# Maximum stage of a graph kernel: positions one group ahead, the other stages one group further behind the messages

## The reference

```python
ew = 1.0 / (pos[src] - pos[dst])
def _graph_conv(x, src, dst, ew, W_rel, b_rel, W_root):
    msg = x[src] * ew[:, None]
    agg = jax.ops.segment_max(msg, dst, num_segments=N)
    agg = jnp.where(jnp.isfinite(agg), agg, 0.0)
    return agg @ W_rel.T + b_rel + x @ W_root.T
```

## Time and profile before

| what | us |
|---|---|
| median of three timed runs | 6097.28 |
| the profiled execution | 6076.85 |
| its span | 6075.1 |
| busy in the span: TensorE | 3609.1 |
| VectorE | 3319.1 |
| GpSimd | 2684.2 |
| ScalarE | 1849.9 |

### The profile page before, as it was taken

The page is one execution under the profiler, slowest core; times in us unless marked ns, Lnnn a source line. Parts: engine busy times, 40 slices in busy tenths (PEclk is TensorE's granted clock), DMA queues, the critical chain, the costliest instruction groups (busy, mean ns, idle before and its releaser), DMA issues. The chain is left out here.

```text
span 6075.1 us, 87448 instructions
## 1 busy us (share of the span) xinstructions
PE 3609.1 (59%) x18318; PEld 2628.9 (43%) x18319; DVE 3319.1 (55%) x10385; ACT 1849.9 (30%) x4701; POOL 2684.2 (44%) x2677
## 2 busy tenths in 40 slices
PE   1455555555554454577214997995666666666664
PEld 0444454455532222244001554654555555555552
DVE  6666666666664444587001333225666666666668
ACT  0444444444422222243000000003444444444442
POOL 1555555555526666601774000005555455454524
PEclk9855555555566676687556998997777777777776
DMA  5555555556531111123103885644333333333331
GB/s 116 182 183 190 186 182 188 185 181 194 185 106 50 49 49 49 49 90 84 22 0 64 200 191 186 196 140 115 87 85 84 83 85 85 84 86 82 87 85 33
DMA packets 822107, 695.48 MB, mean 114 GB/s; under 512 B 538545, under 2 KB 717733, under 8 KB 808431
## 3 DMA queue, kind: packets, MB, share of 16 engines
q1 hardware_dynamic: 552746, 449.58, 24.9%
q0 software_dynamic: 97584, 175.68, 10.8%
q10 hardware_dynamic: 171540, 68.00, 4.7%
HBM read 510.64 MB, written 108.55 MB: 102 GB/s over the span
## 5 line engine op out<-in xcount | busy, mean ns | idle before, releaser
L2362 POOL DMA_INDIRECT ring<-xl_rows,idx x880 | 893.0, 1015 | 1681.1 <-DVE idx L2542 861.6
L435 POOL DMA_INDIRECT ringa<-x_sign_pos,idxa x880 | 864.7, 983 | 691.5 <-DVE msga L600 385.0
L987 POOL DMA_INDIRECT edge_counts<-edge_cnt,places x832 | 828.1, 995 | 733.9 <-issue 262.9
L520 PE MATMUL sela<-hota,endsa 128*128 128x128 f32 x1760 | 425.0, 417 | 482.6 <-ACT endsa L461 400.7
L1905 PE MATMUL pss<-x3s,mats 128*128 128x385 bf16 x2401 | 452.5, 340 | 355.3 <-issue 349.3
L2487 PE MATMUL zps<-xr,hotT 128*128 x2640 | 384.2, 254 | 381.1 <-DVE z L2561 212.6
L520 PEld LDWEIGHTS sela<-hota,endsa 128*128 128x128 f32 x1760 | 365.1, 307 | 500.5 <-issue 430.6
L2500 PE MATMUL ops<-val,hot 128*128 128x200 f32 x1760 | 469.6, 417 | 141.9 <-issue 125.5
L2683 DVE TENSOR_TENSOR out<-out,ops 128x200 f32 x880 | 317.9, 361 | 415.5 <-remote 277.0
L2489 PE MATMUL zps<-We,eaT 128*128 128x128 f32 x1760 | 495.3, 367 | 63.0 <-issue 62.4
L2487 PEld LDWEIGHTS zps<-xr,hotT 128*128 128x128 bf16 x2640 | 271.8, 114 | 492.1 <-issue 458.8
(11 more groups left out here) (388 smaller groups left out, 6591.7 us busy)
## 6 DMA issues: line engine op xcount, KB each, us to landing
edge_counts<-zeroa SPq DMA_DIRECT2D x55, 1568.0 KB
matd<-edge_counts SPq DMA_DIRECT2D x12, 6272.0 KB
keyb<-edge_keys SPq DMA_DIRECT2D x50, 1216.0 KB
reseta<-resets SPq DMA_DIRECT2D x110, 512.0 KB
dstba<-dst_in_tile_bf ACTq DMA_DIRECT2D x112, 256.0 KB
dstb<-dst_in_tile_bf SPq DMA_DIRECT2D x110, 256.0 KB
eaT<-in_eaT SPq DMA_DIRECT2D x880, 32.0 KB
val<-in_ea ACTq DMA_DIRECT2D x880, 32.0 KB
```

Of the source, the lines that this page charges most:

```text
L435: p.indirect_dma_start(out=ring[:, k, :], out_offset=None, in_=table, in_offset=bass.IndirectOffsetOnAxis(ap=idx[:, k:k + 1], axis=0)).the ...
L520: ins = t.matmul(sel[q % 2][:, k * P:(k + 1) * P], ends[:, q % 2, k, :], hot[:, q, k, :], start=True, stop=True)
L987: p.indirect_dma_start(out=g.M.rearrange("d s -> (d s)").unsqueeze(1), out_offset=bass.IndirectOffsetOnAxis(ap=g.place[:, c:c + 1], axis=0 ...
L2362: p.indirect_dma_start(out=ring[:, q % GR, k, :], out_offset=None, in_=g.xl_rows[0:N, :], in_offset=bass.IndirectOffsetOnAxis(ap=idx[:, (q ...
```

## The change

All stages behind the messages move one group further back: in step G, TensorE selects for G-4 (before G-3), transposes the messages of G-2 (G-1) and transposes back G-3 (G-2); VectorE adds G-5 (G-4), scans G-3 (G-2) and loads the tile numbers of G-4 (G-3); the `hot` masks are made for G-1 (G); ScalarE copies G-3 (G-2). The positions of a group are computed by TensorE one step earlier, G+1 in step G, between the message transposes and the transposes back. The gathers, the messages, the distances and the signs stay in their steps. Two turns instead of one stand outside TensorE's and VectorE's loops, and one step more follows VectorE's.

```diff
--- before.py
+++ after.py
@@ -416,6 +416,12 @@
             zero = m.sb(f"zero{tag}", [P, NT * P], BF16)
             s_zero, s_clear = m.sem(f"s_zero{tag}"), m.sem(f"s_clear{tag}")
 
+        def late_turns(eng, body):
+            for it in range(2):
+                body(it)
+            with eng.Fori(2, TURNS) as it:
+                body(it)
+
         with nc.Block() as block:
             @block.gpsimd
             def _(p):
@@ -494,10 +500,10 @@
                             ins = s.activation(sgn[:, q % 2, k, :], ring[:, q * GS + k, F:2 * F], ACT.Copy,
                                                scale=zs[:, q % 2, k:k + 1])
                         ins.then_inc(s_sg, 1)
-                        if not (isinstance(it, int) and q < 2):
-                            ends_of(G - 2, (q - 2) % NG)
+                        if not (isinstance(it, int) and q < 3):
+                            ends_of(G - 3, (q - 3) % NG)
                 turns(s, body, TURNS)
-                for b in (2, 1):
+                for b in (3, 2, 1):
                     ends_of(TURNS * NG - b, NG - b)
                 for h in range(2):
                     s.wait_ge(s_b[h], 16 * (TURNS + 1))
@@ -543,17 +549,18 @@
                 def body(it):
                     for q in range(NG):
                         G = it * NG + q
-                        positions(G, q)
-                        for lag, stage in ((3, select), (1, transposed), (2, back)):
-                            if not (isinstance(it, int) and q < lag):
+                        for lag, stage in ((4, select), (2, transposed), (-1, positions), (3, back)):
+                            if not (isinstance(it, int) and G < lag):
                                 stage(G - lag, (q - lag) % NG)
-                turns(t, body, TURNS)
+                positions(0, 0)
+                late_turns(t, body)
                 GL = TURNS * NG
-                select(GL - 3, NG - 3)
-                transposed(GL - 1, NG - 1)
-                back(GL - 2, NG - 2)
+                for b in (2, 1):
+                    select(GL - b - 2, (-b - 2) % NG)
+                    transposed(GL - b, NG - b)
+                    back(GL - b - 1, (-b - 1) % NG)
+                select(GL - 2, NG - 2)
                 back(GL - 1, NG - 1)
-                select(GL - 2, NG - 2)
                 select(GL - 1, NG - 1)
 
             @block.vector
@@ -607,24 +614,21 @@
 
 
                     G = it * NG + q
-                    first = isinstance(it, int) and it == 0
-                    on = lambda lag: lag >= last and not (first and q < lag)
+                    on = lambda lag: lag >= last and not (isinstance(it, int) and G < lag)
                     at = lambda lag: (G - lag, (q - lag) % NG)
-                    new, adds, msgs = on(0), on(4), on(1)
+                    new, adds, msgs = on(0), on(5), on(1)
                     if adds:
                         A = [v.snap(r, min_val=0, max_val=NT - 1) for r in aregs]
                         for k in range(GS):
-                            add(*at(4), k, A)
-                    if new:
-
-                        wait(v, s_sel, G - NG + 1)
-
-                        v.tensor_tensor(hot[:, q, :, :], bc_mid(g.iota_n[:, :], GS),
-                                        bc_last(g.dend[:, bass.ds(G * GS, GS)], P), ALU.is_equal).then_inc(s_hot, 1)
-                    if on(2):
-                        scan(*at(2), it if q >= 2 else it - 1, ((q - 2) % NG) // 2)
+                            add(*at(5), k, A)
+                    if msgs:
+                        wait(v, s_sel, G - NG)
+                        v.tensor_tensor(hot[:, (q - 1) % NG, :, :], bc_mid(g.iota_n[:, :], GS),
+                                        bc_last(g.dend[:, bass.ds((G - 1) * GS, GS)], P), ALU.is_equal).then_inc(s_hot, 1)
                     if on(3):
-                        load_tiles(G - 3)
+                        scan(*at(3), it if q >= 3 else it - 1, ((q - 3) % NG) // 2)
+                    if on(4):
+                        load_tiles(G - 4)
                     if new:
                         v.wait_ge(s_at, G + 1)
                         v.tensor_reduce(posd[:, :], where[q % 2][:, 0:3 * GS].rearrange("p (k i) -> p k i", i=3), AX.X, ALU.add
@@ -657,8 +661,8 @@
                 def body(it):
                     for q in range(NG):
                         step(it, q)
-                turns(v, body, TURNS)
-                for q in range(4):
+                late_turns(v, body)
+                for q in range(5):
                     step(TURNS, q, q + 1)
```

## The result

The changed kernel took 6139.82 us (four runs, 6135.24 to 6153.99) beside 6096.74 us for the kernel before (four runs): a ratio of 1.0079, 95% interval 1.006 to 1.0097 (intervals below are of the same kind). It is slower by 0.8%, where 5997 us and "faster" were forecast. The time lies inside the range and on the other side of no change.

The account below looks back on a forecast made before the run. Waits on late TensorE results, no full engine, were taken to bound the Maximum stage. Groups of 6.44 to 6.92 us gave -158 to -53 us, middle -105, +5 for drain and code: 5997 us from 6097.28; range 5880 to 6185 us.

Parts of the forecast that it names:

- What bounds the kernel: Maximum stage: no engine fills the 7.14 us a group; VectorE waits 2.05 us; TensorE's late back transposes cost 1.5 us.
- Margins on VectorE: Most of VectorE's 209.2 us wait before positions and 75.0 us before the scan goes, perhaps half of the additions' wait.
- all four signs: VectorE waits: positions under 60 us, scan near 0, the rest before additions; ScalarE's idle before copying back in the hundreds.
- Lateness carried over unchanged: Delay from back's drawn end on TensorE until its result is usable, taken as 1.5 us a group after the change too.
- The sum: Maximum stage: TensorE's recurring cycle 4.94 us plus 1.5 us of late results, 6.44 us a group, -158 us in all.
- bad case: Back, now last in TensorE's step, late by 1.98 us a group: 6.92 us a group, -53 us in all.
- Positions ahead of back: On TensorE, position matmuls enter the recurring cycle ahead of back, adding 0.29 us a group.
- calm cycle: Copy, select, transposes, back, next copy when nothing is late: 4.65 us before, 4.94 us forecast after the change.
- The slower one: Rival, chance 0.22: GpSimd's gathers hold TensorE's results; margins lengthen runs to twelve, 7.55 us a group, +86 us, 6183 us.
- Everything hidden: Rival, chance 0.12: TensorE waits less and runs more at 2.4 GHz; 5.3 us a group, -409 us, 5690 us.
- No change: Rival, chance 0.16: back late by 2.1 to 2.3 us a group eats the other gains; within 18 us of 6097.

Follow-up runs that it names:

- lag_only: The changed kernel with the positions of G back at the head of TensorE's step, directly behind back: 6016.84 us, ratio 0.9994 to the kernel before.
- the exchange alone: The kernel before with only the positions of G+1 put ahead of back of G-2, no distance changed: 6057.84 us, ratio 1.0057.
- before_paced: The kernel before, with GpSimd waiting ahead of each four gathers until the four before have landed: 6514.39 us, ratio 1.067.
- after_paced: The changed kernel, with GpSimd waiting ahead of each four gathers until the four before have landed: 6488.78 us, ratio 1.0632 to the kernel before.

## Why the prediction was wrong

*What bounds the kernel*: right as far as it went. TensorE's late results, not its busy time, set the pace, and VectorE's own 5.09 us step is about what is left without them (5.23 to 5.33 us a group without gathers). Naming the cause was put off as "not in the profile", and that is where it went wrong.

*Margins on VectorE*: right. Positions under 60 us (23.7), scan near 0 (14.2), ScalarE's idle in the hundreds, remaining waits before the additions: all four signs that I had named for "right" appeared, and the time went the other way. They showed that the waits would move, not that they would shrink. The additions didn't lose half of their wait but got over three times as much, 361.5 instead of 110.7 us, of which the prediction had counted 50.7 us.

*Lateness carried over unchanged*: the step that failed. The sum was 4.94 + 1.5 = 6.44 us, in its bad case 4.94 + 1.98 = 6.92 us, both with a lateness read from the unchanged kernel. By the semaphore updates lateness of back rose by 2.69 - 1.89 = 0.80 us. Added to the sum that gives 7.24 us, near the measured 7.31, but the nearness is partly luck: with the cycle and the lateness as measured the same sum is 4.83 + 2.69 = 7.52 us, and for `lag_only` 4.65 + 2.85 = 7.50 us against 7.01 us, since not every copy waits for a late result. Lateness is not independent of the change. In `lag_only`, with the distances alone, it rose to 2.85 us, and the time stayed where it was. The likely chain is that GpSimd issues as long as the ring has free places and the margins let VectorE free them earlier; but longer runs aren't all of it, since with runs capped at eight lateness was 2.55 us. The order of the work also moved back's results to 3 to 5 us into a run, where 45 of 51 were late and none had fallen before. Which of the two makes how much isn't shown.

*Positions ahead of back*: seen, priced at 0.29 us a group, and outweighed on paper by the gains. Measured 0.18 us in the calm cycle and 0.57% for the exchange alone, 34 us or 0.16 us a group. As the gains were nothing, this small term became the result.

*The rivals.* The slower one had the right mechanism for the first half: runs of twelve, many copies about 2 us after their end, three groups in 1030.33 - 1009.07 = 21.3 us where I had worked out 22.6. It overrated the price (7.55 us a group), since 34 of the runs, not all, are of twelve. Its rule that held results wait until GpSimd stops holds for about half of them, and results in the first four gathers of a run of eight or twelve, prompt by its reading, were late in 45 of 70 cases; and by `lag_only` runs of twelve alone don't make the kernel slower. Its chance of 0.22 was too low: the trace had shown the hold twice, and the bounds for a cost that depends on the change should not have been taken from the unchanged kernel. Everything hidden fell although the clock rose to 0.68. No change is what the distances by themselves gave.

The Trainium skill (SBUF - State Buffer, "Who interferes with whom"), by which the slower rival falls, states that TensorE and ScalarE never wait on anyone at SBUF's ports. The runs don't contradict it for ports, but it can't be read as saying that TensorE's results don't depend on GpSimd: with gathers they are late by 1.9 to 2.7 us in the mean, without by 0.01 us.

Open: by what path gathers hold TensorE's results. A break in issuing ends it, an instruction of 0.12 us doesn't, and plain loads of as many bytes don't cause it. Also open: why the exchange cost nothing that could be seen where a break of 0.76 us stood beside it, with results still held.

## What to carry to other kernels

Before adding slack to a pipeline, ask what the slack sets free: here a producer that runs ahead as far as the ring allows, and whose running ahead goes with longer waits. A delay taken from the old trace may be carried into a sum only if what causes it is known not to move. Of two steps side by side in a queue, the one on the recurring cycle goes first, however short the other is.

## What the runs showed of the hardware

- While GpSimd issues indirect gathers back to back, results of TensorE become usable late. Results of back that ended in the first 2 us of a run of eight or twelve were prompt (66 of 66 in the two kernels), later than 5.1 us they were all late (102 of 102), and between 3 and 5 us 45 of 51. About half of the late ones came after the last gather of the run, most of these 1 to 2.5 us behind it; the others came earlier, while GpSimd still issued.
- A break of 1.40 us behind each four gathers ends it for back, 1.08 us mostly (37 of the 97 groups that could be told over 1 us, 40 of all 220 by the copies' starts), 0.92 us partly (1.59 us in the mean), 0.76 us not (2.06 us), though the time fell by 0.7%. Doing nothing for 1.08 us made this kernel 3.4% faster.
- GpSimd, waiting for four gathers of 128 rows to land, stood 3.95 us in the median in `before_paced` and 2.96 us in `after_paced`.
